# Mask products of a graph-attention kernel in column tiles: halves in layer 1, strips in layers 0 and 2

## What is computed

```
e = leaky_relu(u[:, None] + v[None, :] + c, 0.2)
scores = where(adj > 0, e, -9e15)
att = softmax(scores, axis=1)
h_next = elu(att @ features)
```

## Time and profile before

| | |
|---|---|
| Time, median of 3 runs | 3651.12 us (3648.79 to 3652.38) |
| Profiled execution, its own time | 3647.5 us |
| Its span, first to last instruction | 3645.6 us |
| TensorE busy | 3300.6 us, 91% (18817 matmul records) |
| VectorE busy | 2885.4 us, 79% |
| ScalarE busy | 2241.4 us, 61% |
| GpSimd busy | 117.3 us, 3% |
| Granted TensorE clock, mean | 0.976 |

### The profile page before, as it was taken

The page is one execution under the profiler, slowest core; times in us unless marked ns, Lnnn a source line. Parts: engine busy times, 40 slices in busy tenths (PEclk is TensorE's granted clock), DMA queues, the critical chain, the costliest instruction groups (busy, mean ns, idle before and its releaser), DMA issues. The chain is left out here.

```text
span 3645.6 us, 49985 instructions
## 1 busy us (share of the span) xinstructions
PE 3300.6 (91%) x18817; PEld 1077.3 (30%) x18961; DVE 2885.4 (79%) x5283; ACT 2241.4 (61%) x3933; POOL 117.3 (3%) x138
## 2 busy tenths in 40 slices
PE   1689999999999997999999999979999999999998
PEld 0323222322323233323232323224333233232322
DVE  5478888888888864889898989876887788778876
ACT  0356667766667673667676767654655665566555
POOL 0000000000000000000000000000000000000000
PEclk9989999999999997999999999988999999999999
DMA  8999999999999911121212121121112112111200
GB/s 256 284 356 346 332 332 336 330 340 340 334 331 337 317 67 58 60 100 59 100 65 94 69 96 70 61 110 44 60 63 84 68 54 82 66 68 54 82 31 6
DMA packets 414084, 578.19 MB, mean 159 GB/s; under 512 B 294402, under 2 KB 315010, under 8 KB 389266
## 3 DMA queue, kind: packets, MB, share of 16 engines
q1 hardware_dynamic: 409458, 564.40, 47.9%
q0 software_dynamic: 4384, 10.59, 1.0%
HBM read 430.10 MB, written 77.69 MB: 139 GB/s over the span
## 5 line engine op out<-in xcount | busy, mean ns | idle before, releaser
L553 ACT ACTIVATE prob<-eps,v2col 128x512 f32<-128x512 f32 x3072 | 1927.5, 689 | 971.7 <-PE eps L711 969.9
L1101 DVE SCALAR_TENSOR_TENSOR eps<-ua,v8col,cb 128x512 f32<-128x512 f32 x2800 | 1980.6, 754 | 487.0 <-ACT prob L553 477.3
L754 PE MATMUL acc<-prob,feat 128*64 128x512 f32 x6144 | 1514.9, 615 | 0.0
L711 PE MATMUL eps<-nt,nbig 128*128 128x512 fp8e4 x3072 | 924.5, 385 | 171.8 <-DVE eps L1101 143.0
L754 PEld LDWEIGHTS acc<-prob,feat 128*64 128x64 f32 x6144 | 379.5, 138 | 743.1 <-issue 492.8
L763 PE MATMUL den<-prob,ones 128*32 128x512 f32 x4096 | 545.8, 605 | 0.0
L711 PEld LDWEIGHTS eps<-nt,nbig 128*128 128x128 bf16 x3072 | 276.8, 100 | 861.7 <-DVE eps L1101 607.0
L940 DVE TENSOR_SCALAR mi<-stage 128x1024 uint8<-128x1024 int32 x512 | 352.1, 689 | 63.7 <-DMA stage<-in_adj_dram 63.5
L949 DVE TENSOR_SCALAR edges<-nt 128x2048 int32<-128x2048 int32 x192 | 234.3, 1220 | 32.7 <-PE misc L721 18.9
L721 PE MATMUL misc<-edges,oneh 128*32 128x512 fp8e4 x3072 | 192.6, 394 | 70.6 <-DVE edges L949 55.9
L763 PEld LDWEIGHTS den<-prob,ones 128*32 128x32 f32 x4096 | 80.6, 108 | 418.0 <-issue 418.0
(11 more groups left out here) (154 smaller groups left out, 1233.2 us busy)
## 6 DMA issues: line engine op xcount, KB each, us to landing
stage<-in_adj_dram SPq DMA_DIRECT2D x512, 512.0 KB, 6.2
nt<-nt_d SPq DMA_DIRECT2D x128, 1024.0 KB, 5.0
nt_d<-nt SPq DMA_DIRECT2D x64, 1024.0 KB, 7.1
ub<-u_d SPq DMA_DIRECT2D x48, 256.0 KB, 5.3
xy_d<-xin POOLq DMA_DIRECT2D x32, 256.0 KB, 3.0
xin<-xy_d SPq DMA_DIRECT2D x32, 256.0 KB, 2.9
nt<-mi SPq DMA_TRANSPOSE x256, 6.7
xin<-in_x_dram SPq DMA_DIRECT2D x16, 128.0 KB, 5.9
```

The source lines that it names most:

```text
L553: nc.scalar.activation(prob[:, j % TS, :], eps[:, j % ES, :], ACT.Exp, bias=v2col[:, j:j + 1]).then_inc(s_p, 1)
L711: nc.tensor.matmul(et, nbig[:, :], half_block(nt[:, par, m, :], m, o), start=False, stop=True, skip_group_check=True).then_inc(s_z, 1)
L754: mm = nc.tensor.matmul(acc[h:h + C, :], feat[:, l % 2, j, 0:C], prob[:, j % TS, :], start=(k == 0), stop=(k == NT // 2 - 1))
L1101: dv.scalar_tensor_tensor(eps[:, j % ES, :], ua[:, par, :], v8col[:, j:j + 1], cb[:, par, :], ALU.add, ALU.max).then_inc(s_fill, 1)
```

## The change

`mask_scores` gets a number of columns, `cols`, and makes the mask product of a tile as 128 / `cols` products one after another: `nbig[:, c:c + cols]` with the same mask, into the partitions c to c + cols of the same bank, each in its own column tile. The last one signals ScalarE. The product of ones in layer 0 is cut in the same way.

The new function `mask_cols` sets the columns for each tile. It takes the four tiles between two bursts of sums together. If the tail or the head puts one of TensorE's listed steps between those bursts (t = 8, 24, 27, 29 and, in layers 0 and 1, 31; t = 47, 56, 57; in the first block of a layer all t up to 21), the four stay whole (128). Otherwise it takes `MASK_COLS`: 32 in layers 0 and 2, 64 in layer 1. The steps that count edges are not in the list. Nothing else changes: no instruction of another engine, no transfer, no wait. In the whole program 1340 of the 3072 mask products become four strips each, 640 become two halves and 1092 stay whole; of the 272 products of ones 176 become four strips. TensorE issues 18122 matmuls instead of 12934, each with its load of weights.

```diff
--- before.py
+++ after.py
@@ -48,6 +48,7 @@
 ES = 5
 AHEAD = 3
 LAGQ = 1
+MASK_COLS = (32, 64, 32)
 
 ACT_TILES = ((2, 5), (), ())
 ON_ACT = tuple(frozenset(j for j in range(AHEAD, NT) if j % 7 in ks) for ks in ACT_TILES)
@@ -699,17 +700,33 @@
                 on_act = j in ON_ACT[l]
                 pe.wait_ge(s_filla if on_act else s_fill, started(l, b, j, on_act))
 
-            def mask_scores(l, b, j, par):
+            def mask_cols(l, j, head, tail):
+
+                first = j // QUAD * QUAD - 1
+                whole = []
+                if tail:
+                    whole += [T_TURN, T_HT, T_OUT, T_OUT + 2] + [T_OUT + 4] * (l < 2)
+                else:
+                    whole += range((NT + 2) // 3)
+                if head:
+                    whole += [T_FOLD, T_HEADT, T_ROWS]
+                return P if any(first <= t < first + QUAD for t in whole) else MASK_COLS[l]
+
+            def mask_scores(l, b, j, par, cols):
 
                 on_act = j in ON_ACT[l]
                 et = eps[:, j % ES, :]
+                m, o = divmod(j, MT)
+                edge = half_block(nt[:, par, m, :], m, o)
                 if on_act:
 
-                    nc.tensor.matmul(et, onesb[:, :], mrow[:, par, :], start=False, stop=False,
-                                     skip_group_check=True)
-                m, o = divmod(j, MT)
-                nc.tensor.matmul(et, nbig[:, :], half_block(nt[:, par, m, :], m, o), start=False, stop=True,
-                                 skip_group_check=True).then_inc(s_z, 1)
+                    for c in range(0, P, cols):
+                        nc.tensor.matmul(et[c:c + cols, :], onesb[:, c:c + cols], mrow[:, par, :], start=False,
+                                         stop=False, skip_group_check=True, tile_position=(0, c))
+                for c in range(0, P, cols):
+                    mm = nc.tensor.matmul(et[c:c + cols, :], nbig[:, c:c + cols], edge, start=False, stop=True,
+                                          skip_group_check=True, tile_position=(0, c))
+                mm.then_inc(s_z, 1)
 
             def count_edges(l, b, m):
 
@@ -856,7 +873,7 @@
                         if tail and t == T_HT:
                             pe.wait_ge(s_h, blk(l, b))
                         wait_started(l, b, t)
-                        mask_scores(l, b, t, par)
+                        mask_scores(l, b, t, par, mask_cols(l, t, head, tail))
                         if t % QUAD == QUAD - 1:
                             k = t // QUAD - LAGQ
                             if k >= 0:
```

## The result

The changed kernel takes 3604.31 us (median of 4 runs, 3602.57 to 3605.63) against 3651.18 us before: a ratio of 0.9872 (95% interval 0.9855 to 0.9889), 46.9 us less. The forecast was 3608 us.

What follows compares the result with a forecast made beforehand. TensorE was taken to lead in layer 2, with VectorE nearly as full in layer 1. Savings of 14 (layer 2), 13 (layer 1), 12 (clock) and 4 us (layer 0) sum to 43 us, giving 3608 us, range 3582 to 3638 us.

Steps and rivals of the forecast that it cites:

- The chain on TensorE in layer 2: In layer 2 TensorE leads; what it saves anywhere but at the head's row maxima, the block saves.
- quads 10 and 13: Layer-2 groups of mask products (quad k: tiles 4k to 4k+3) held by VectorE; no saving ahead of them.
- The price of a width: On TensorE, each change of column width between neighbouring products costs about 0.10 to 0.11 us.
- Layer 2: Strips in 11 quads of a middle block save 0.88 us a block; 14 us in the layer.
- the 0.02 us behind strips: Step from strips to sums stays a width change, about 0.02 us longer than behind 128-wide work.
- Layer 1: Halves in ten quads save 0.89 us a block, 13 us for 15 blocks; VectorE covers quads 2 to 5.
- The clock: Layer 1's half-clock stretches behind the head, 1.55 us a block: half of 23 us saved, 12 us.
- Layer 0: Four of ten strip quads (9, 11, 15, 1) gain, less ten 0.02 us steps: 0.28 us a block, 4 us.
- No change: Rival: the 0.11 us belongs to something else, or strips' weights come late; 3640 to 3655 us; chance 0.07.
- the clock stays: Rival: every layer-1 block keeps its slow stretch, or gets a second; 3620 us or a little over; chance 0.20.
- more: Rival: VectorE's steps move with TensorE, so quads called covered gain too; 76 us less, 3575 us; chance 0.13.
- supply of instructions: Rival: over 65 ns per TensorE instruction makes layers 0 and 2 grow; about 3705 us at 67 ns; chance 0.10.

Runs made afterwards that it cites:

- e5: The change with strips of 32 columns in layer 1 too, instead of halves: 3624.18 us, ratio 0.9933 to the kernel before.
- e1: Strips in layer 2 alone, mask products of layers 0 and 1 whole: 3633.13 us, ratio 0.9961 to the kernel before.
- e7: The change plus six unused products, in halves, in each layer-1 block where TensorE waits behind the head: 3589.55 us, ratio 0.9838 to the kernel before.
- e8b: The kernel before plus six unused whole products in each layer-1 block, run again for an undisturbed profile: 3625.25 us, ratio 0.9935.
- e3: Strips in layer 0 alone, mask products of layers 1 and 2 whole: 3641.73 us, ratio 0.9982 to the kernel before.
- e9: The change with each layer-2 strip cut once more into two products of 256 mask columns: 3605.70 us, ratio 0.9880 to the kernel before.
- e6: The change without its exception, so halves and strips next to tail and head steps too: 3612.80 us, ratio 0.9903 to the kernel before.
- e10: The change with halves in all layers, six unused products per layer-1 block, and strips (tiles 56, 57) or halves (58, 59) around the head's turn and spread: 3568.61 us.
- e2: Halves in layer 1 alone, mask products of layers 0 and 2 whole: 3625.19 us, ratio 0.9941 to the kernel before.
- e4: The change with halves of 64 columns in layers 0 and 2 too, instead of strips: 3589.81 us, ratio 0.9842 to the kernel before.

## Why the prediction was right

**What bounds.** The chain on TensorE in layer 2 held. By the distances between the bursts of sums, nine of the eleven strip quads of a block are 0.10 to 0.11 us shorter; quads 10 and 13, which the prediction had left out, aren't.

**The price of a width.** 0.11 us was forecast ahead of strips; the rows have 0.12 (0.88 us instead of 1.00, 1.72 instead of 1.84). The product groups hold the 0.216 us that was assumed. e5 shows that it is the neighbour's width that counts and not the size of the piece. The Trainium skill's drain at a change of tiling (TensorEngine Tiling (Array Packing), Key Properties) has the sign right; the fast weight load that column tiling turns off by the same page (Restrictions) cost at most 0.01 us on the path: a strip quad needs 0.98 us to the sums instead of 0.97.

**Layer 2**: 14 us forecast, 15.2 found, 14.2 alone in e1; blocks 71.0 for 71.05. Of the 0.02 us behind strips the step to the sums shows 0.01 and the sums 0.01. Quad 10 is held by VectorE as forecast: its strips take 1.10 us instead of 0.98, by this timeline of PE.

```profile
2918.81 1.17 PE L727 MATMUL eps<-nt,nbig 128*32 128x512 fp8e4 x16
2919.91 0.65 PE L771 MATMUL acc<-prob,feat 128*64 128x512 f32 x2
```

**Layer 1**: 13 us for the width, 12 to 14 found; blocks of 59.05 and 60.7 us for "59 and 60.5". VectorE works without a pause where I had it cover the saving. The terms were less exact than their sum, by the distances between bursts of sums in e7 against e8b, both without slow stretches: quads 3 to 6 gave 0.10 us for 0.15, quads 9 to 12 0.25 for 0.30, quads 13 and 14 0.15 as forecast, quad 15 0.21 for 0.10 and quad 1 0.17 for 0.25.

**The clock**: half of 23 us, 12, was a choice between two ends and not a result. It was 8 to 10 us: six of fifteen stretches went. That it came near the middle is luck. That it can be bought outright by six idle products (e7, e8b) was not in the prediction.

**Layer 0** was mis-sized, 4 us forecast and 7.4 found in the whole change, 6.2 in e3. The middle block gained 0.48 us (849.7 / 11 against 844.4 / 11) and not 0.28. "Of ten strip quads I count four whose first step is on the path" missed a fifth: quad 4, which was put among those behind waits for VectorE, waits for nothing, neither before (first two rows) nor with the change, and its first step falls from 1.00 to 0.88 us.

```profile
570.98 1.07 PE L763 MATMUL den<-prob,ones 128*32 128x512 f32 x8
571.98 0.39 PE L708 MATMUL eps<-mrow,onesb 128*128 128x512 bf16 x1
569.09 1.06 PE L780 MATMUL den<-prob,ones 128*32 128x512 f32 x8
569.97 0.40 PE L724 MATMUL eps<-mrow,onesb 128*32 128x512 bf16 x4
```

And "less some ten steps of 0.02 us" was too much: quads 1, 4, 9, 11 and 15 are each 0.11 us shorter with the later start of the sums included, and the rest together lose some 0.05 us.

**The sum.** 43 us forecast, 44.8 found in the span. Layers 0 and 2 gave 3.4 and 1.2 us more than their terms, the clock 2 to 4 us less; that these cancel to 2 us is luck. The mechanism, and which engine leads where, held.

**The rivals.** No change and "the clock stays" are refuted by the result and by nine stretches for fifteen; "more" asked for 0.8 us a block in layer 0 and 1.32 in layer 2, which isn't there. The slower one, supply of instructions at more than 65 ns, is refuted by the result as well: 7788 + 7805 records in 994.0 us are one in 64 ns, and the blocks got shorter. e9 took the rate to 48 ns without a loss.

The step that a reader should mark is one that I left out: for layers 0 and 2 I costed what the change saves at one side of the mask products and never compared it with the other side. The rows for that stood in the earlier trace rows: the step to the sums, and their first pair, 0.15 us together in layer 1 against 0.11 for the step ahead.

## What to carry to other kernels

Look for the distance between the starts of neighbouring matmul groups, and compare the same group behind different neighbours: what differs here is the change of column tiling, about 0.1 us each time. Give a cheap product the width of the neighbour whose start is the most expensive to delay, here the float32 sums, and check the price of a step in such a pair on both sides. Where another engine paces, saved TensorE time turns into waits; a few idle products in the longest of them kept the clock up in layer 1 and were worth 12 to 15 us on top of the change's 47.

## What the runs showed of the hardware that I had not expected

- A transpose of bf16 with 3 columns of weights stands in the tiling of strips: strips before and behind it ran without a pause (e6, e10), while whole products had 0.32 us ahead of it instead of 0.22. The float32 transpose with 64 columns (L836) doesn't: in e6 it starts 0.33 us behind strips, in the changed kernel 0.22 us behind a whole product.
- The slow clock hangs together with the length of the block. Before, each block of layer 1 was 61.4 us long and had one slow stretch; with the width alone (e2) blocks of 59.05 and 60.7 us alternate irregularly. 1.5 to 1.6 us were lost each time, with TensorE at 1.2 GHz for about 3.4 us.
- The weights of the first float32 pair behind a change of width come about 0.05 us late, and in time when the width stays: 1.81 us for four pairs up to the denominators, against 1.87. Single records show it. Before, the pair's loads start with the pair (3023.71 us), and the next pair comes 0.48 us later; in e4 they start 0.21 us ahead of it, and the next pair comes 0.43 us later.
